# The two value products of an attention tile on two column halves of TensorE, their parts summed at the head's end

## The chip, the cores and the metric

One NeuronCore of a Trainium2 chip runs the program. The metric is the device time of one execution in microseconds. The engines are named as in the profile: PE is TensorE (PEld its weight loads), DVE VectorE, ACT ScalarE, POOL GpSimd, SP the engine that issues most DMAs.

## The reference, cut to what matters

```python
q, k, v = (split_heads(x @ W + b) for W, b in ((Wq, bq), (Wk, bk), (Wv, bv)))   # B=2, L=4096, 16 heads of 16
scores = einsum('bhqd,bhkd->bhqk', q, k) * scale
sparsity = scores.max(-1) - scores.mean(-1)
_, top_idx = top_k(sparsity, 307)
q_sel = take_along_axis(q, top_idx)                       # 307 queries a head
attn = softmax(einsum('bhud,bhkd->bhuk', q_sel, k) * scale)
out_sel = einsum('bhuk,bhkd->bhud', attn, v)              # the two value products
out = zeros_like(q).at[bi, hi, top_idx].set(out_sel)
x = layernorm(x + out.reshape(b, l, D) @ Wo + bo)
x = layernorm(x + rwkv_channel_mix(x))                    # a small gated feed-forward block
```

There are 32 heads in all (two batches of 16). Each has a full score pass, whose row maxima pick 307 queries, and then an attention pass for those 307 over all 4096 keys.

## The kernel before

**The score pass** of a head takes 64 steps. In each, PE makes 128 queries by 2048 scores: one 512-column product into bank `C0` (L782, issued ahead as "lead"), one into `C1` (L791), and two into a half of `DP` (L801). ACT takes absolute values of `C0` and `C1` into `AB` (L1035, two a step), and one DVE instruction adds `DP` and `AB` and keeps the maximum (L1185, followed by the read of its accumulator). `C0` and `C1` have one buffer each, so PE may write the next L782 only when ACT has read the last. 2048 such steps run from about 63 to 2943 us.

**The attention pass** of a head takes 32 tiles of 128 keys. For a tile PE makes 128 keys by 307 scores in bank `B` (L862), ACT takes the exponential into `E` in f32 (L1064), and POOL (or DVE in the last stretch) writes `EL`, what is left of `E` beyond its upper 16 bits. `EH` is a bf16 view of these upper bits. Six tiles later PE multiplies both by the same values: `v` holds 16 columns of the f16 upper part of V, 16 of its lower part and one column of ones. Both products add up in the one bank `PV`, over all 32 tiles:

```python
v = V[hx // H][0][:, (kc * H + h) * VW:(kc * H + h) * VW + 128]
pe.matmul(PV[:, 0:U], v, EH[a % NE], start=kc == 0, stop=False)
pe.matmul(PV[:, 0:U], v, EL[a % NE], start=False, stop=kc == NT - 1).then_inc(pv_pe, 1)
```

The 128 columns of `v` are 33 useful ones and 95 of neighbouring heads, whose results nobody reads.

**The head's end**: ACT copies 33 rows of `PV` to `OT` (L1071), PE transposes them in three pieces (L887), DVE takes the reciprocal of the ones' row, adds the two value parts and multiplies (L1353, L1354, L1356, L1359), and POOL adds the bias and scatters the rows to `AO`.

**The order of the work** is written out ahead by `schedule()`: one list of tokens that every engine walks through, each doing its own part. One score step takes one step of the selection (`sel`: flip, 16 rounds of compare and count, ranks, indices) and one step of the attention. In the steady part PE's order is L782 (next step), L877, L878, L791, L801 twice, L862. Selection steps hold the attention back for a step or two, so a head whose tiles fall into a search takes more score steps. After the last score step ("tail") the attention of the last heads runs alone, and then the feed-forward block of the second batch.

One place outside the attention matters for the reading. The product of the selection's indices (`idx`, L850) has 32 products with `n * 20` columns of weights: 100 for groups of five heads, 60 for groups of three.

Of the kernel before, what the change touches and what calls it, by code (L numbers as in the profile page):

```python
# [9 lines left out]
ALU = mybir.AluOpType  # L10
ACT = mybir.ActivationFunctionType

NB, L, D, H, DH = 2, 4096, 256, 16, 16
NT = L // 128
U = max(1, min(512, int(0.6 * 512)))
# [12 lines left out]
NE = 10  # L28
# [10 lines left out]
def after(engine, semaphore, value):  # L39

    if value > 0:
        engine.wait_ge(semaphore, value)
# [392 lines left out]
def attention_rwkv(nc, x, Wq, bq, Wk, bk, Wv, bv, Wo, bo, W_r, W_k, W_v, mu_r, mu_k, out):  # L435
    ctx = ExitStack()
    with ctx:
        def sb(name, shape, dt=F32):
            return ctx.enter_context(nc.sbuf_tensor(name, shape, dt))

        def sem(name):
            return ctx.enter_context(nc.semaphore(name))
# [8 lines left out]
        VW = 2 * DH + 1  # L451
# [4 lines left out]
        V = [(VF, VS), (XT, XV.rearrange("p t (h d) -> p t h d", d=VW))]  # L456
# [6 lines left out]
        EH = [E[i][:].bitcast(BF16).rearrange("p (u w) -> p u w", w=2)[:, :, 1] for i in range(NE)]  # L463
        W2 = {n: sb("W_" + n, [128, 2, D]) for n in ("k", "o", "rT", "kT", "vT")}
        WH = {n: (sb(f"W{n}h", [128, 2, D], F16), sb(f"W{n}l", [128, 2, D], F16)) for n in ("k", "q", "v")}
        ident = sb("ident", [128, 128])
# [26 lines left out]
        EL = [SCR[:, 6936 + 154 * i:7090 + 154 * i].bitcast(F16)[:, 0:U] for i in range(NE)]  # L493
# [36 lines left out]
        idxs = [sb(f"idxs{i}", [128, HM, 3], I32) for i in range(len(GROUPS))]  # L530
        MH = sb("MH", [128, 24])
        QT = [sb(f"QT{i}", [128, 384], F16) for i in range(2)]
        OT = [sb(f"OT{i}", [2 * DH + 1, 384]) for i in range(2)]
        rec = sb("rec", [128, 3])
        osum = sb("osum", [128, 3, DH])
        OG = [sb(f"OG{i}", [128, 3, DH]) for i in range(2)]

        FF = VF[:, 0:NT * H * VW].bitcast(F32)
# [2 lines left out]
        def ff_tiles(count, w=D):  # L541
# [17 lines left out]
        PV = ctx.enter_context(nc.psum_tensor("PV", [128, 512], F32))  # L559
        DP = ctx.enter_context(nc.psum_tensor("DP", [128, 2, 1024], F32))  # L560
        BANK = {"C0": CP[:, 0, :], "C1": CP[:, 1, :], "B": BP[:], "P": PV[:], "D0": DP[:, 0, :], "D1": DP[:, 1, :],
                "D00": DP[:, 0, 0:512], "D01": DP[:, 0, 512:1024], "D10": DP[:, 1, 0:512], "D11": DP[:, 1, 512:1024]}
# [26 lines left out]
        pv_pe, ot_act, ot_pe, og_dve = (sem(n) for n in ("pv_pe", "ot_act", "ot_pe", "og_dve"))  # L589
# [11 lines left out]
        for token in plan:  # L601
            if token[0] == "st":
                a = (HEAD0[token[1]] + token[2]) * NT + token[3]
# [70 lines left out]
        def _(pe):  # L674
            owed = {}

            def claim(bank):
                banks = {"D0": ("D0", "D00", "D01"), "D1": ("D1", "D10", "D11"), "D00": ("D00", "D0"), "D01": ("D01", "D0"),
                         "D10": ("D10", "D1"), "D11": ("D11", "D1")}.get(bank, (bank,))
                for b in banks:  # L680
                    for s, v in owed.pop(b, ()):
                        pe.wait_ge(s, v)
                return BANK[bank]
# [182 lines left out]
            def pv(g, hl, kc):  # L866
                hx = HEAD0[g] + hl
                a, h = hx * NT + kc, hx % H
                if kc == 0:
                    claim("P")  # L870
                    pe.wait_ge(val_pool, 32 * (hx // H + 1))
                    if hx // H:
                        pe.wait_ge(vones_pool, 1)
                on, count = low[a]
                pe.wait_ge(el_of[on], count)
                v = V[hx // H][0][:, (kc * H + h) * VW:(kc * H + h) * VW + 128]
                pe.matmul(PV[:, 0:U], v, EH[a % NE], start=kc == 0, stop=False)  # L877
                pe.matmul(PV[:, 0:U], v, EL[a % NE], start=False,  # L878
                          stop=kc == NT - 1).then_inc(pv_pe, 1)
                owed["P"] = ((ot_act, hx + 1),)  # L880

            def otr(g, hl, bank):
                hx = HEAD0[g] + hl
                o = claim(bank)
                pe.wait_ge(ot_act, hx + 1)
                for c in range(3):
                    r = pe.transpose(o[:, 64 * c:64 * c + 2 * DH + 1], OT[hx % 2][:, 128 * c:128 * c + 128],  # L887
                                     ident[0:2 * DH + 1, 0:2 * DH + 1])
                r.then_inc(ot_pe, 1)
                owed[bank] = ((og_dve, hx + 1),)  # L890

# [49 lines left out]
            def f7(b, t, c, bank, late):  # L941
# [5 lines left out]
                if c == 1:  # L947
                    r.then_inc(f_v, 1)
                    owed[bank] = ((f_o1, k + 1),)

            stages = dict(xt=xt, kbar=kbar, ffw=ffw, kmm=kmm, qmm=qmm, qtr=qtr, val=val, lead=lead_, second=second, main=main, flip=flip, cnt=cnt, cut=cut, rank=rank,
                          idx=idx, st=st, pv=pv, otr=otr, f1=f1, f2=f2, f4=f4, f6=f6, f6k=f6k, f7=f7)
            for stage, *args in plan:
                if stage in stages:
# [3 lines left out]
        def _(act):  # L958
            seq = Seq(q_act)
# [106 lines left out]
            def fin(g, hl):  # L1066
                hx = HEAD0[g] + hl
                after(act, ot_pe, hx - 1)
                act.wait_ge(consts, 2)
                act.wait_ge(pv_pe, NT * (hx + 1))  # L1070
                act.copy(OT[hx % 2][:, 0:U], PV[0:2 * DH + 1, 0:U]).then_inc(ot_act, 1)  # L1071

            def f1(b, t, bank, late):
                k = NT * b + t
# [37 lines left out]
            def f6k(b, t, part, bank, late):  # L1112
# [6 lines left out]
                if late:  # L1119
                    after(act, f_v, k - 1)  # L1120
                    act.wait_ge(f_rl, k + 1)
                    act.activation(fk2[k % 2], fk[k % 2], ACT.Square).then_inc(f_sq, 1)

            stages = dict(xtev=xtev, ffw=ffw, kev=kev, split=split, qev=qev, qtev=qtev, vev=vev, main=main, flip=flip, cmp=cmp, st=st, fin=fin,
                          f1=f1, f2s=f2s, f4=f4, f6=f6, f6k=f6k)
            for stage, *args in plan:
# [4 lines left out]
        def _(dve):  # L1131
            seq = Seq(q_dve)
# [214 lines left out]

            def otr(g, hl, bank):
                hx = HEAD0[g] + hl
                sv = BANK[bank][:, 0:192].rearrange("p (c d) -> p c d", c=3)  # L1350
                dve.wait_ge(ot_pe, hx + 1)
                after(dve, og_dve, hx)
                dve.reciprocal(rec[:], sv[:, :, 2 * DH])  # L1353
                q = seq.mark(dve.tensor_copy(osum[:], sv[:, :, 0:DH]))  # L1354
                dve.wait_ge(q_dve, q)
                q = seq.mark(dve.tensor_tensor(osum[:], osum[:], sv[:, :, DH:2 * DH], ALU.add))  # L1356
                dve.wait_ge(q_dve, q)
                after(dve, l_o[hx % 2], 48 * (hx // 2))
                dve.tensor_tensor(OG[hx % 2][:], osum[:], rec[:].unsqueeze(2).broadcast_to([128, 3, DH]),  # L1359
                                  ALU.mult).then_inc(og_dve, 1)  # L1360
# [67 lines left out]
            def f9(b, t, late):  # L1428
                if late:
# [6 lines left out]
            stages = dict(xtev=xtev, kbar=kbar, kev=kev, split=split, main=main, cap=capture, parts=parts, cmp=cmp,  # L1436
                          digit=digit, cut=cut, cum=cum, rank=rank, pick=pick, slots=slots, ob=ob, oa=oa, idx=idx,
                          st=st, otr=otr, f2=f2, f3=f3, f5=f5, f7=f7, f8=f8, f9=f9)
            for stage, *args in plan:
                if stage in stages:  # L1440
# [3 lines left out]
        def _(pool):  # L1444
# [5 lines left out]
            def setup():  # L1450
# [23 lines left out]
                for i in range(2):  # L1474
                    q = seq.mark(pool.memset(OT[i][:], 1.0))
                pool.wait_ge(q_pool, q)
# [198 lines left out]
            def put(g, hl):  # L1675
# [5 lines left out]
                pool.wait_ge(og_dve, hx + 1)  # L1681
                pool.wait_ge(q_pool, seq.mark(pool.tensor_tensor(OG[i][:], OG[i][:], bv3, ALU.add)))
                pool.wait_ge(l_z, 256)
                for c, (_, w) in enumerate(CH):
                    k = 3 * hl + c
                    pool.indirect_dma_start(  # L1686
                        out=AOr[b], out_offset=bass.IndirectOffsetOnAxis(ap=ixf[0:w, k:k + 1], axis=0),
                        in_=OG[i][0:w, c, :], in_offset=None).then_inc(l_o[i], 16)

# [262 lines left out]
```

## Time and profile before

| | us |
|---|---|
| median of 3 runs | 3242.62 (3241.13 to 3245.9) |
| profiled execution, its time | 3246.53 |
| profiled execution, its span | 3244.8 |
| PE busy | 2945.3 (91%) |
| DVE busy | 2894.6 (89%) |
| ACT busy | 2821.5 (87%) |
| POOL busy | 1611.0 (50%) |

The span is from the first instruction to the last. A matmul's duration in the profile is modelled and includes the way through the array, so that back-to-back matmuls overlap in the rows. What a matmul costs is read from the distance of its start to the start of the next one: 0.22 us for 512 columns, 0.13 for 307, at full clock.

### The profile page before, as it was taken

The numbers are of one execution on the slowest core, as the hardware profiler recorded it, in microseconds if no ns is written. First come the engines' busy times: TensorE is split into PE (matmuls) and PEld (weight loads), VectorE is DVE, ScalarE is ACT, GpSimd is POOL, SyncE is SP. The second block draws the span as 40 slices with busy tenths as digits, with TensorE's granted clock in tenths as the row PEclk, the third lists the DMA queues.
The fourth block names the chain that finished last, engine by engine and source line by source line (L and its number), as shares of the span: only waits on it lengthen the run. The fifth ranks groups of instructions, "written<-read, shape, count | busy, mean of one in ns | idle before, by whom it ended". The sixth has DMA issues, their size and how long they took to land. (4 is left out here: it accounts for less than half of the span.)

```text
span 3244.8 us, 56078 instructions
## 1 busy us (share of the span) xinstructions
PE 2945.3 (91%) x14524; PEld 1334.2 (41%) x14524; DVE 2894.6 (89%) x5704; ACT 2821.5 (87%) x6214; POOL 1611.0 (50%) x2867
## 2 busy tenths in 40 slices
PE   6999899998999999999899999899998799897588
PEld 3333333333433433443343444444444343344376
DVE  4999999999989998998999999899998698997567
ACT  5999898998999999999899888799997699895476
POOL 4223022224645554653364566766546464657754
PEclk8999999999999999999999999999999999998889
DMA  6324223241251242123111252122241212202122
GB/s 183 92 84 119 74 72 86 86 41 34 44 42 29 37 42 36 21 39 36 35 37 44 51 46 51 38 39 36 42 48 38 46 33 20 42 17 16 19 84 74
DMA packets 276909, 166.61 MB, mean 51 GB/s; under 512 B 182188, under 2 KB 256108, under 8 KB 272492
## 3 DMA queue, kind: packets, MB, share of 16 engines
q1 hardware_dynamic: 268492, 159.56, 26.0%
q0 software_dynamic: 6144, 1.37, 0.5%
q8 instruction: 117, 1.92, 0.3%
q10 hardware_dynamic: 1952, 2.10, 0.2%
q14 instruction: 204, 1.67, 0.2%
HBM read 111.86 MB, written 47.86 MB: 49 GB/s over the span
## 5 line engine op out<-in xcount | busy, mean ns | idle before, releaser
L1185 DVE CUSTOM_DVE_ANT_0 JK<-DP,AB 128x1024 bf16<-128x1024 f32 x2048 | 2459.6, 1222 | 215.2 <-DVE SPr L1185 88.6
L1035 ACT ACTIVATE AB<-CP 128x512 f32<-128x512 f32 x4096 | 2292.1, 623 | 188.5 <-PE CP L782 131.1
L801 PE MATMUL DP<-KS,QS 128*128 128x512 f16 x4096 | 1233.5, 383 | 69.1 <-DVE SPr L1185 60.8
L1673 POOL TENSOR_TENSOR SCR<-E 128x307 f16<-128x307 f32 x957 | 665.1, 708 | 491.4 <-ACT E L1064 485.4
L782 PE MATMUL CP<-KS,QS 128*128 128x512 f16 x2048 | 791.4, 386 | 56.3 <-ACT AB L1035 33.0
L791 PE MATMUL CP<-KS,QS 128*128 128x512 f16 x2048 | 792.2, 387 | 36.3 <-ACT AB L1035 0.2
L801 PEld LDWEIGHTS DP<-KS,QS 128*128 128x128 f16 x4096 | 354.4, 99 | 368.7 <-DVE SPr L1185 179.1
L1064 ACT ACTIVATE E<-BP 128x307 f32<-128x307 f32 x896 | 428.5, 478 | 40.3 <-PE BP L862 34.4
L782 PEld LDWEIGHTS CP<-KS,QS 128*128 128x128 f16 x2048 | 197.6, 96 | 532.8 <-ACT AB L1035 457.9
L791 PEld LDWEIGHTS CP<-KS,QS 128*128 128x128 f16 x2048 | 196.8, 96 | 421.1 <-ACT AB L1035 375.2
L862 PE MATMUL BP<-QT,KA 128*128 128x307 f16 x896 | 265.7, 297 | 12.4 <-DMA QT<-SCR 8.6
L1448 POOL TENSOR_SCALAR SCR<-SCR 128x48 f16<-128x48 f16 (+2 forms) x122 | 50.1, 410 | 388.1 <-ACT SCR L1013 190.9
L1185 DVE DVE_READ_ACCUMULATOR2_ANT SPr<- 128x1 f32 x2048 | 168.1, 82 | 0.0
L877 PE MATMUL PV<-E,XT 128*128 128x307 bf16 x512 | 158.8, 311 | 6.6 <-POOL SCR L1673 6.2
L878 PE MATMUL PV<-SCR,XT 128*128 128x307 f16 x512 | 155.3, 304 | 0.0
L877 PE MATMUL PV<-E,VF 128*128 128x307 bf16 x512 | 153.0, 299 | 0.0
L878 PE MATMUL PV<-SCR,VF 128*128 128x307 f16 x512 | 149.6, 292 | 0.0
L862 PEld LDWEIGHTS BP<-QT,KA 128*128 128x128 f16 x896 | 88.0, 98 | 142.9 <-ACT E L1064 27.5
L1646 POOL DMA_INDIRECT SCR<-QN,idxs x96 | 99.5, 1037 | 70.5 <-DMA idxs<-IDX 34.3
L1686 POOL DMA_INDIRECT AO<-OG,idxs x96 | 100.5, 1047 | 33.9 <-issue 20.5
L1064 ACT ACTIVATE E<-DP 128x307 f32<-128x307 f32 x100 | 40.9, 429 | 51.8 <-PE DP L862 48.5
L1711 POOL TENSOR_SCALAR frs<-fmv 128x1 f32<-128x1 f32 x64 | 14.1, 220 | 136.4 <-DVE fmv L1369 135.9
(411 smaller groups left out, 3016.9 us busy)
## 6 DMA issues: line engine op xcount, KB each, us to landing
KS<-KTC SPq DMA_DIRECT2D x256, 128.0 KB
QS<-QSC SPq DMA_DIRECT2D x512, 64.0 KB
KA<-KTC SPq DMA_DIRECT2D x128, 128.0 KB
QN<-SCR SPq DMA_DIRECT2D x16, 544.0 KB, 3.4
SCR<-in_L_attn_x SPq DMA_DIRECT2D x16, 512.0 KB, 5.1
AO<-E SPq DMA_DIRECT2D x16, 512.0 KB, 6.8
VF<-in_L_attn_x SPq DMA_DIRECT2D x64, 128.0 KB, 2.1
VF<-AO SPq DMA_DIRECT2D x64, 128.0 KB, 2.2
```

The costliest lines, as they stand in the source:

```text
L782: pe.matmul(o, qs, ks[0][:, 1, :], start=True, stop=True).then_inc(sc_c, 1)
L791: pe.matmul(o, qs, ks[1][:, 1, :], start=True, stop=True).then_inc(sc_c, 1)
L801: r = pe.matmul(o[:, 512 * j:512 * j + 512], qs, ks[j][:, 0, :], start=True, stop=True)
L862: pe.matmul(o[:, 0:U], KA[hx % 2][:, 128 * kc:128 * kc + 128], QT[hx % 2][:, 0:U], start=True, stop=True).then_inc(s_pe, 1)
L877: pe.matmul(PV[:, 0:U], v, EH[a % NE], start=kc == 0, stop=False)
L878: pe.matmul(PV[:, 0:U], v, EL[a % NE], start=False, stop=kc == NT - 1).then_inc(pv_pe, 1)
L1035: act.activation(AB[p % 3][:, 512 * j:512 * j + 512], BANK["C%d" % j], ACT.Abs).then_inc(ab_full, 1)
L1064: act.activation(E[a % NE][:], BANK[bank][:, 0:U], ACT.Exp, scale=2 * SCALE / (WS * WS)).then_inc(ex_act, 1)
L1185: dve.tensor_tensor_reduce(out=JK[p % 2][:], in0=BANK["D%d" % u], in1=AB[p % 3][:], scale=1.0, scalar=0.0, op0=ALU.add, op1=ALU.max, accum ...
L1646: pool.indirect_dma_start(out=QG[0:w, 3 * (hx % 8) + c, :], out_offset=None, in_=QNr[b], in_offset=bass.IndirectOffsetOnAxis(ap=ixf[0:w, k ...
L1673: pool.tensor_tensor(EL[a % NE], E[a % NE][:], EH[a % NE], ALU.subtract).then_inc(el_g, 1)
L1686: pool.indirect_dma_start(out=AOr[b], out_offset=bass.IndirectOffsetOnAxis(ap=ixf[0:w, k:k + 1], axis=0), in_=OG[i][0:w, c, :], in_offset= ...
```

## The change

The two value products of a tile no longer add up in the same rows. Each takes 64 columns of weights instead of 128. The product with `EH` goes to rows 0 to 63 of `PV`, the one with `EL` to rows 64 to 127, each accumulated over the 32 tiles by itself. At the head's end ACT copies all 128 rows, PE transposes 128 rows (three products of 128 columns instead of 33), and DVE sums what were one denominator and two value parts from two denominators and four value parts. `rec` now comes from `den`.

```diff
-        OT = [sb(f"OT{i}", [2 * DH + 1, 384]) for i in range(2)]
+        OT = [sb(f"OT{i}", [128, 384]) for i in range(2)]
+        den = sb("den", [128, 3])
...
-                v = V[hx // H][0][:, (kc * H + h) * VW:(kc * H + h) * VW + 128]
-                pe.matmul(PV[:, 0:U], v, EH[a % NE], start=kc == 0, stop=False)
-                pe.matmul(PV[:, 0:U], v, EL[a % NE], start=False,
-                          stop=kc == NT - 1).then_inc(pv_pe, 1)
+                v = V[hx // H][0][:, (kc * H + h) * VW:(kc * H + h) * VW + 64]
+                pe.matmul(PV[0:64, 0:U], v, EH[a % NE], start=kc == 0, stop=kc == NT - 1)
+                pe.matmul(PV[64:128, 0:U], v, EL[a % NE], start=kc == 0, stop=kc == NT - 1).then_inc(pv_pe, 1)
...
-                    r = pe.transpose(o[:, 64 * c:64 * c + 2 * DH + 1], OT[hx % 2][:, 128 * c:128 * c + 128],
-                                     ident[0:2 * DH + 1, 0:2 * DH + 1])
+                    r = pe.transpose(o[:, 128 * c:128 * c + 128], OT[hx % 2][:, 128 * c:128 * c + 128], ident[:])
...
-                act.copy(OT[hx % 2][:, 0:U], PV[0:2 * DH + 1, 0:U]).then_inc(ot_act, 1)
+                act.copy(OT[hx % 2][:, 0:U], PV[:, 0:U]).then_inc(ot_act, 1)
...
-                sv = BANK[bank][:, 0:192].rearrange("p (c d) -> p c d", c=3)
+                sv = BANK[bank][:, 0:384].rearrange("p (c a e) -> p c a e", c=3, a=2)
+                parts = sv[:, :, :, 0:2 * DH].rearrange("p c a (b d) -> p c d a b", d=DH)
                 dve.wait_ge(ot_pe, hx + 1)
                 after(dve, og_dve, hx)
-                dve.reciprocal(rec[:], sv[:, :, 2 * DH])
-                q = seq.mark(dve.tensor_copy(osum[:], sv[:, :, 0:DH]))
+                q = seq.mark(dve.reduce_sum(den[:], sv[:, :, :, 2 * DH], mybir.AxisListType.X))
+                dve.reduce_sum(osum[:], parts, mybir.AxisListType.XY)
                 dve.wait_ge(q_dve, q)
-                q = seq.mark(dve.tensor_tensor(osum[:], osum[:], sv[:, :, DH:2 * DH], ALU.add))
+                q = seq.mark(dve.reciprocal(rec[:], den[:]))
```

No instruction changes its place, and the number of instructions of each engine stays. On PE, in a steady score step with attention, these rows stood before (columns of weights by columns streamed; `E` and `SCR` are `EH` and `EL`, `VF` is V of the first batch):

```order
L782 MATMUL CP<-KS,QS 128x512
L877 MATMUL PV<-E,VF 128x307
L878 MATMUL PV<-SCR,VF 128x307
L791 MATMUL CP<-KS,QS 128x512
L801 MATMUL DP<-KS,QS 128x512 x2
```

The same place of PE's program after the change (one line was added to the file above it, so each line number is one higher):

```order
L783 MATMUL CP<-KS,QS 128x512
L878 MATMUL PV<-E,VF 64x307
L879 MATMUL PV<-SCR,VF 64x307
L792 MATMUL CP<-KS,QS 128x512
L802 MATMUL DP<-KS,QS 128x512 x2
```

Nothing moved: the two value products stand between the same two score products, now with 64 columns of weights while their neighbours have 128.

On DVE, at a head's end, these four rows stood before (`BP` is the bank with the transposed `OT`):

```order
L1353 RECIPROCAL rec<-BP 128x3
L1354 COPY osum<-BP 128x48
L1356 TENSOR_TENSOR osum<-osum,BP 128x48
L1359 TENSOR_TENSOR OG<-osum,rec 128x48
```

The same place on DVE after the change:

```order
L1353 TENSOR_REDUCE den<-BP 128x3
L1354 TENSOR_REDUCE osum<-BP 128x48
L1356 RECIPROCAL rec<-den 128x3
L1359 TENSOR_TENSOR OG<-osum,rec 128x48
```

Four small instructions remain four; two of them now reduce out of PSUM, and the reciprocal comes after the sum.

## Rows read from the trace of the kernel before

**Rows 1.** Busy time by engine: five steady heads, then a head during a search

```profile
2102.60:2327.40 224.80, 223.16 (x1175) 95.62 (x1175) 212.76 (x359) 221.73 (x504) 138.38 (x211) 1.00 0.23 42
1219.00:1286.50 67.50, 63.50 (x307) 24.64 (x306) 59.78 (x137) 65.02 (x148) 28.23 (x49) 1.00 0.10 19
```

**Rows 2.** The same view for L1185 alone, in the second stretch

```profile
1219.00:1286.50 67.50, 55.29 (x92) 1.00 0.10 19
```

**Rows 3.** Timeline of one steady score step with attention: start, duration, engine, line

```profile
2908.11 0.29 PE L862 MATMUL BP<-QT,KA 128*128 128x307 f16 x1
2908.26 0.39 PE L782 MATMUL CP<-KS,QS 128*128 128x512 f16 x1
2908.48 0.30 PE L877 MATMUL PV<-E,XT 128*128 128x307 bf16 x1
2908.50 0.51 ACT L1064 ACTIVATE E<-BP 128x307 f32<-128x307 f32 x1
...
2908.62 0.29 PE L878 MATMUL PV<-SCR,XT 128*128 128x307 f16 x1
...
2908.75 0.39 PE L791 MATMUL CP<-KS,QS 128*128 128x512 f16 x1
2908.82 1.17 ACT L1035 ACTIVATE AB<-CP 128x512 f32<-128x512 f32 x2
2908.82 1.22 DVE L1185 CUSTOM_DVE_ANT_0 JK<-DP,AB 128x1024 bf16<-128x1024 f32 x1
2908.97 0.59 PE L801 MATMUL DP<-KS,QS 128*128 128x512 f16 x2
...
2909.41 0.29 PE L862 MATMUL BP<-QT,KA 128*128 128x307 f16 x1
```

**Rows 4.** L877 alone by stretch: PE busy (x tiles), weight loads, granted clock

```profile
821.00:1763.00 942.00, 152.71 (x511) 50.34 (x511) 1.00 0.25 36
2103.00:2943.00 840.00, 106.42 (x355) 35.06 (x355) 0.98 0.23 36
2943.00:3080.00 137.00, 52.34 (x157) 16.59 (x157) 0.80 0.21 17
```

**Rows 5.** PE's timeline around an index product with 100 columns of weights

```profile
791.39 0.60 PE L801 MATMUL DP<-KS,QS 128*128 128x512 f16 x2
791.83 1.76 PE L850 MATMUL BP<-SCR 128*100 128x80 f16 x32
793.43 0.38 PE L782 MATMUL CP<-KS,QS 128*128 128x512 f16 x1
```

**Rows 6.** PE's timeline around an index product with 60 columns of weights

```profile
1601.62 0.60 PE L801 MATMUL DP<-KS,QS 128*128 128x512 f16 x2
1602.15 1.36 PE L850 MATMUL PV<-SCR 128*60 128x48 f16 x32
1603.45 0.39 PE L782 MATMUL CP<-KS,QS 128*128 128x512 f16 x1
```

**Rows 7.** PE's timeline in the tail, at half clock and then at full

```profile
3028.44 0.46 PE L877 MATMUL PV<-E,XT 128*128 128x307 bf16 x1
...
3029.21 0.46 PE L877 MATMUL PV<-E,XT 128*128 128x307 bf16 x1
...
3032.92 0.30 PE L877 MATMUL PV<-E,XT 128*128 128x307 bf16 x1
3033.05 0.29 PE L878 MATMUL PV<-SCR,XT 128*128 128x307 f16 x1
...
3033.31 0.30 PE L877 MATMUL PV<-E,XT 128*128 128x307 bf16 x1
```

**Rows 8.** A head's end: OT's transposes, osum's copy, and 128-column transposes elsewhere

```profile
L887 PE MATMUL BP<-ident,OT x87: 217/224/248, 864.3 to 3078.6; 33*128 33x33 f32 x87
L1354 DVE COPY osum<-BP x29: 165/176/179, 866.0 to 3079.0; 128x48 f32<-128x48 f32 x29
L687 PE MATMUL PV<-ident,SCR 128*128 128x128 f32 x100 | 16.8, 295 | 9.8 <-DMA SCR<-in_L_attn_x 7.6 <-issue 2.1
```

## The prediction

> **What bounds the kernel now.** I read the busy time by stretch first, then the timeline of single steps. Over five steady attention heads PE is busy 223.16 of 224.80 us, ACT 221.73 and DVE 212.76, at granted clock 1.00 (the 2.4 GHz level) [rows 1]. The reader is to see that three engines are nearly full there, and PE fullest. Busy matmul time is modelled and overlaps, so I check it in the timeline [rows 3]: from L862 to the next L862 is 1.30 us, and PE's starts follow each other without a hole: 0.15 (L862 to L782), 0.22 (to L877), 0.14 (to L878), 0.13 (to L791), 0.22 (to L801), 0.44 (two L801). A 307-column product needs 0.13 and a 512-column one about 0.22, so all that is slack in 1.30 us is some 0.02 before L782, 0.01 in the L877 distance and little else. Whatever is added to PE in such a step is added to the step, less about 0.02.
>
> Where a search runs, it is different: 67.50 us for a head's 32 tiles [rows 1], with 92 rows of L1185 [rows 2], two a step, so 46 steps of 1.47 us. Here steps without a tile and waits of the search lie between, and part of an addition disappears in them.
>
> Tiles by stretch: 511 + 355 = 866 beside score steps, and 157 in the tail, where the granted clock averages 0.80 [rows 4] (one record is missing from 1024). In the tail the score steps are gone and PE often sets the pace alone: a tile takes 3033.31 - 3032.92 = 0.39 at full clock, which is three products of 0.13, and 3029.21 - 3028.44 = 0.77 at half clock [rows 7].
>
> **The change, part by part.** *The pair itself.* Before, both products stream one after the other through the whole array: 0.14 + 0.13 = 0.27 [rows 3]. Two halves of the array could stream them together. From below, the second starts with the first and the pair costs 0.13 (-0.14); from above, they still go one after the other and cost 0.27 (0). I take a value near the lower bound: the second starts one weight load later. The nearest row is the 60-column index product, whose 32 loads and products follow each other at (1603.45 - 1602.15 - 0.10)/32 = 0.04 [rows 6]. So the pair costs 0.04 + 0.13 = 0.17, a gain of 0.10. No row here shows two halves working at once.
>
> *Entering and leaving the half-width form.* PE goes from 128 columns of weights to 64 and back in every tile. The index product does the same with 60 columns and, for the larger groups, not with 100. With 100 columns L801's pair to L850 is 791.83 - 791.39 = 0.44, two plain 512-column distances [rows 5]; with 60 it is 1602.15 - 1601.62 = 0.53 [rows 6]. Entering costs 0.09. Leaving: the 60-column group ends at 1602.15 + 1.36 = 1603.51, its last product is about 0.19 long, so it starts at 1603.32, and L782 follows 0.13 later, though 48 columns stream in 0.02 at the rate of rows 3 (0.13 for 307). With 100 columns the same distance is 793.59 - 0.21 = 793.38 to 793.43, 0.05. Leaving thus costs 0.08 to 0.11; I take 0.10. That is 0.19 a tile, seen in every row pair of this kind and to be hidden only where PE waits anyway. On this the Trainium skill (TensorEngine Tiling (Array Packing), Key Properties) says that changing the tiling mode, and not only the tile, drains TensorE. By that rule each tile pays twice; the trace agrees, with 0.09 and 0.10 us. The page gives no price.
>
> *Sum for a steady step.* 0.19 - 0.10 = +0.09 on the stretch from L782 to L791, +0.01 as the weight load of L791 can't run ahead, -0.02 of slack: +0.08, from 1.30 to 1.38. Sixteen of the 27 heads beside score steps run like the first stretch of rows 1, about 512 tiles: 512 x 0.08 = 41 us. The other 354 tiles lie in searches; I count half: 14. Together 55.
>
> *Tail.* A tile goes from 0.39 to 0.13 + 0.09 + 0.04 + 0.13 + 0.10 = 0.49, +0.10. About half of 157 tiles are paced by PE at full clock (80 x 0.10 = 8), some 25 at half clock with twice the price (5): 13.
>
> *The head's end, 32 times.* PE's three transposes take 128 columns of f32 instead of 33: modelled durations 295 against 224 ns [rows 8], at most +0.21 a head, 7 us; but the 33-row form seems to be entered and left at a price too, about 0.19, 6 us, and goes. I take 0, and -6 to +7 as its ends. DVE: a copy is 176 ns [rows 8]; two copy-like instructions become reductions over 6 and 192 elements. From 0 to one more copy's time each, 0 to 11 us in all, hidden behind PE except where PE waits for the bank; I take 2. ACT's copy of 128 rows instead of 33 has the same 307 elements a row: 0. If the cover of the last head is gone, these are a few tenths of a us.
>
> Nothing else moves: POOL, the DMAs and every wait stay.
>
> Sum: 55 + 13 + 2 = 70; I take 66, since ACT and DVE get slack and catch up after searches. Against the profiled execution that is 3246.53 + 66 = 3313. The median of the runs is 3.9 lower: 3309. Since a pair somewhat shorter than I took it is as likely as not, I say 3305, which is +62.
>
> **Rivals.** *One after the other (0.17).* The halves don't overlap. The pair stays at 0.27 and both entries are paid in full: +0.19 - 0.02 = +0.17 a step. (512 + 177) x 0.17 = 117, tail 80 x 0.19 + 25 x 0.38 = 25: +142, 3385. For it: the second product's weights are loaded only after the first has been issued. Against: nothing makes the second product wait for the first.
>
> *Faster (0.05).* Entering and leaving costs nothing beside long neighbours, because the 0.09 and 0.10 of the index product come from its short products, and only the overlap is left: -0.10 to -0.14 a tile. It decides where the switch price falls under 0.10. ACT (221.73 of 224.80 [rows 1]) then sets the step, so that only 0.02 is gained in 689 steps (14), and in the tail 80 x 0.08 = 6: -20, 3223. Against: the 0.09 of entering follows a 512-column product, just as here [rows 6]. The Trainium skill (TensorEngine Tiling (Array Packing), Theoretical Speedup) gives up to two times for products with at most 64 columns of weights, which points this way; by that rule alone the pair would cost 0.13. Here it is the mechanism of this rival without the switches, and no row before shows it.
>
> *No difference (0.04).* The switches cost about what the overlap gives (-0.14 + 0.16), and the slack of 0.02 hides it: 3242.6.
>
> *The clock (0.05).* Twice 0.1 us without a stream in each 1.4 us step, and the granted clock, 1.00 in steady heads [rows 1], falls to half as it does in the tail [rows 4]. Every twentieth of the 1780 us of attention beside score steps at half clock costs nearly as much again, some 60 to 80 us: 3380 and more. Against: in the search head of rows 1 PE also pauses (63.50 of 67.50 us busy) and the granted clock stays at 1.00.
>
> *As forecast, two switches and an overlap (0.69).* Its own range: second product at once and other slack, +0.04 a step: 28 + 8 = +36, less the head's end, +25 at the lowest, 3268; second product 0.08 later and all of it exposed, +0.12: 83 + 17 = +100, 3340.
>
> **How the numbers follow.** The range has to reach from the lowest of the forecast's cases into the serial rival, whose own low end is about 3350 and middle 3385: 3262 to 3385 leaves out some 0.09 below (faster, none) and 0.09 above. A difference of 0.2% (6.5 us) is about what a measurement of this kernel can tell from none. Faster 0.05, same 0.04, slower 0.91 (0.69 + 0.17 + 0.05).
>
> **What the changed profile would show.** Right: L783 to L792, 0.49 before, is about 0.59; L783 to L878 is 0.31, L878 to L879 is 0.04 or less, L879 to L792 0.23; the steady step is 1.38, with PE's distances leaving no hole and holes appearing on DVE and ACT; in the tail a tile at full clock takes 0.49. Serial rival: L878 to L879 0.13 or more. Faster rival: L783 to L878 stays at 0.22. Clock rival: the granted clock of steady heads under 1.00. The prediction would be wrong most easily in the distance from L878 to L879, for which I have only a neighbour's rows, and next in how much of the addition the searches hide.

## The result: 1.6% slower, and the profile after

| | us |
|---|---|
| before, median of 4 runs | 3243.14 (3241.13 to 3245.9) |
| changed, median of 4 runs | 3294.93 (3289.77 to 3303.08) |
| ratio, with its 95% interval | 1.0157 (1.0133 to 1.0182) |
| changed, profiled execution and its span | 3290.62, 3288.9 |

The change costs 52 us. The profiled execution lies 4.3 below the median and before's 3.4 above it, so that the changed span is only 44.1 longer.

The timeline of PE in a steady step of the changed kernel (start, duration, engine, line), to be held against [rows 3]:

```profile
2240.75 0.29 PE L863 MATMUL BP<-QT,KA 128*128 128x307 f16 x1
2240.88 0.38 PE L783 MATMUL CP<-KS,QS 128*128 128x512 f16 x1
2241.19 0.33 PE L878 MATMUL PV<-E,XT 128*64 128x307 bf16 x1
2241.20 0.32 PE L879 MATMUL PV<-SCR,XT 128*64 128x307 f16 x1
2241.45 0.39 PE L792 MATMUL CP<-KS,QS 128*128 128x512 f16 x1
2241.68 0.59 PE L802 MATMUL DP<-KS,QS 128*128 128x512 f16 x2
2242.11 0.29 PE L863 MATMUL BP<-QT,KA 128*128 128x307 f16 x1
```

The two value products now start 0.01 apart instead of 0.14: the halves stream together. But the first starts 0.31 after L783 instead of 0.22, and L792 starts 0.25 after the second instead of 0.13. From L783 to L792 it is 0.57 instead of 0.49, and the step takes 1.36 instead of 1.30.

Busy time by stretch: its length, then PE, weight loads, DVE, ACT, POOL, then granted clock, DMA share and GB/s. First the five steady heads and the search head of [rows 1], then the tail.

```profile
2120.40:2353.80 233.40, 232.23 (x1174) 87.21 (x1175) 213.56 (x361) 229.88 (x504) 138.48 (x211) 1.00 0.23 41
1226.97:1294.66 67.69, 64.10 (x307) 23.43 (x306) 59.80 (x139) 65.31 (x149) 28.28 (x49) 1.00 0.17 19
2971.00:3124.00 153.00, 113.38 (x549) 43.68 (x549) 79.56 (x216) 65.21 (x157) 103.11 (x164) 0.61 0.24 15
```

The same view of before's tail:

```profile
2943.00:3078.00 135.00, 87.12 (x549) 53.69 (x549) 86.71 (x214) 62.63 (x157) 104.30 (x164) 0.80 0.22 17
```

Five steady heads take 233.40 instead of 224.80 us, 0.054 for each of their 160 tiles. PE is still the fullest engine, at full clock, and DVE has done the same work in more time. The search head, from the start of its first tile to the end of its last, takes 67.69 instead of 67.50, under 0.01 for each of its 32 tiles. The tail grows from 135.0 to 153.0, and its granted clock falls from 0.80 to 0.61.

The score pass by its first and last instruction on DVE, before and then changed (duration min/median/max, first and last start):

```profile
L1185 DVE CUSTOM_DVE_ANT_0 JK<-DP,AB x2048: 1204/1223/1270, 63.6 to 2941.5; 128x1024 bf16<-128x1024 f32 x187
```

```profile
L1184 DVE CUSTOM_DVE_ANT_0 JK<-DP,AB x2048: 1201/1224/1273, 65.5 to 2969.8; 128x1024 bf16<-128x1024 f32 x187
```

It lasts 2904.3 instead of 2877.9 us: +26.4. The start is 1.9 later, the tail is 18 longer, and what follows the tail is some 2 shorter. That makes up the 44. Taken head by head, from a head's first value product to its last, the 26 is made of +28.0 in the sixteen heads without a search (0.055 a tile), +5.6 in ten of the eleven whose tiles fall into a search (0.018 a tile), -5.9 in the eleventh, +1.1 between the heads and -2.4 ahead of the first tile.

The -5.9 doesn't come from the change. Before, one subtraction of DVE took 4.79 us in that head, while POOL worked without a pause beside it:

```profile
2793.70 4.79 DVE L1324 TENSOR_TENSOR SCR<-fa,numbers 128x192 f16<-128x192 f16 x1
```

In the changed kernel it takes 0.35. It is as long in two more kernels with the old form there (`cols96`, `head_end`) and short in two others with the old form there (`tail_only`, `tail_all`), so it is chance that before's profile has it. Without it the score pass would be some 32 us longer, not 26.

The tail of the changed kernel on PE, at half clock and then at full:

```profile
3060.72 0.44 PE L878 MATMUL PV<-E,XT 128*64 128x307 bf16 x1
3060.72 0.47 PE L879 MATMUL PV<-SCR,XT 128*64 128x307 f16 x1
3061.12 0.44 PE L863 MATMUL CP<-QT,KA 128*128 128x307 f16 x1
3061.49 0.47 PE L878 MATMUL PV<-E,XT 128*64 128x307 bf16 x1
...
3062.22 0.32 PE L878 MATMUL PV<-E,XT 128*64 128x307 bf16 x1
...
3062.72 0.33 PE L878 MATMUL PV<-E,XT 128*64 128x307 bf16 x1
```

At full clock a tile takes 0.50 (3062.22 to 3062.72) against 0.39 [rows 7]. At half clock it takes 0.77, exactly as before. Over the tail's distances from tile to tile, before had 80 at 0.39 to 0.42 and 27 at 0.76 to 1.0; now 44 are at 0.43 to 0.50 and 75 at 0.76 to 1.0.

The head's end, changed: DVE's four rows (busy us, mean ns).

```profile
L1353 DVE TENSOR_REDUCE den<-BP 128x3 f32<-128x6 f32 x29 | 4.6, 159 | 2.4 <-PE BP L887 2.1 <-issue 0.3
L1354 DVE TENSOR_REDUCE osum<-BP 128x48 f32<-128x192 f32 x29 | 10.1, 348 | 0.0
L1356 DVE RECIPROCAL rec<-den 128x3 f32<-128x3 f32 x32 | 5.3, 166 | 0.0
L1359 DVE TENSOR_TENSOR OG<-osum,rec 128x48 f32<-128x48 f32 x32 | 6.7, 210 | 1.2
```

The sum over 192 elements takes 348 ns where the copy took 176 [rows 8], and the others are 14 to 37 ns shorter: with before's 174 + 176 + 203 + 224 = 777 in the same view, 883 now, +0.1 us a head. On PE it is the other way round: from the product ahead of the three transposes to the one behind them it takes 0.54 us instead of 0.61 (medians of 27 heads).

### The profile page after: what moved, and what is told of

Same layout as the page of the kernel before. It is cut to its first block and busy times, and to the rows that moved or that the text cites. A ratio compares the mean times of both kernels' runs of the same rounds, so it can differ in the third digit from the quotient of the medians.

```text
span 3288.9 us, 56078 instructions
## 1 busy us (share of the span) xinstructions
PE 3014.1 (92%) x14524; PEld 1280.5 (39%) x14524; DVE 2884.8 (88%) x5704; ACT 2859.9 (87%) x6214; POOL 1608.6 (49%) x2867
## 3 DMA queue, kind: packets, MB, share of 16 engines
q8 instruction: 117, 1.92, 0.3%
## 5 line engine op out<-in xcount | busy, mean ns | idle before, releaser
L1034 ACT ACTIVATE AB<-CP 128x512 f32<-128x512 f32 x4096 | 2250.5, 602 | 186.4 <-PE CP L783 126.3
L783 PE MATMUL CP<-KS,QS 128*128 128x512 f16 x2048 | 785.8, 384 | 53.4 <-ACT AB L1034 32.8
L792 PE MATMUL CP<-KS,QS 128*128 128x512 f16 x2048 | 797.6, 389 | 36.0 <-ACT AB L1034 0.6
L1063 ACT ACTIVATE E<-BP 128x307 f32<-128x307 f32 x896 | 385.3, 430 | 37.1 <-PE BP L863 30.3
L783 PEld LDWEIGHTS CP<-KS,QS 128*128 128x128 f16 x2048 | 198.6, 97 | 444.6 <-ACT AB L1034 318.6
L792 PEld LDWEIGHTS CP<-KS,QS 128*128 128x128 f16 x2048 | 196.8, 96 | 433.6 <-ACT AB L1034 291.8
L878 PE MATMUL PV<-E,XT 128*64 128x307 bf16 x512 | 179.2, 354 | 2.9 <-POOL SCR L1673 2.9
L879 PE MATMUL PV<-SCR,XT 128*64 128x307 f16 x512 | 176.7, 349 | 0.0
L878 PE MATMUL PV<-E,VF 128*64 128x307 bf16 x512 | 166.7, 326 | 0.0
L879 PE MATMUL PV<-SCR,VF 128*64 128x307 f16 x512 | 163.2, 319 | 0.0
L878 PEld LDWEIGHTS PV<-E,VF 128*64 128x64 f16 x512 | 54.6, 107 | 160.3 <-POOL SCR L1673 93.6
L878 PEld LDWEIGHTS PV<-E,XT 128*64 128x64 f16 x512 | 57.2, 112 | 152.7 <-POOL SCR L1673 85.3
```

Source lines behind the costliest of these rows:

```text
L783: pe.matmul(o, qs, ks[0][:, 1, :], start=True, stop=True).then_inc(sc_c, 1)
L792: pe.matmul(o, qs, ks[1][:, 1, :], start=True, stop=True).then_inc(sc_c, 1)
L878: pe.matmul(PV[0:64, 0:U], v, EH[a % NE], start=kc == 0, stop=kc == NT - 1)
L879: pe.matmul(PV[64:128, 0:U], v, EL[a % NE], start=kc == 0, stop=kc == NT - 1).then_inc(pv_pe, 1)
L1034: act.activation(AB[p % 3][:, 512 * j:512 * j + 512], BANK["C%d" % j], ACT.Abs).then_inc(ab_full, 1)
L1063: act.activation(E[a % NE][:], BANK[bank][:, 0:U], ACT.Exp, scale=2 * SCALE / (WS * WS)).then_inc(ex_act, 1)
```

## The experiments

### One half, and the width alone

`one_half` keeps 64 columns of weights, but puts both products into the same half, as before into one sum. `cols96` takes 96 columns. Both have the old head's end. Product rows of `one_half`, with 64 for 96 the only difference to `cols96`:

```diff
-                v = V[...][:, (kc * H + h) * VW:(kc * H + h) * VW + 128]
-                pe.matmul(PV[:, 0:U], v, EH[a % NE], start=kc == 0, stop=False)
-                pe.matmul(PV[:, 0:U], v, EL[a % NE], start=False,
+                v = V[...][:, (kc * H + h) * VW:(kc * H + h) * VW + 64]
+                pe.matmul(PV[0:64, 0:U], v, EH[a % NE], start=kc == 0, stop=False)
+                pe.matmul(PV[0:64, 0:U], v, EL[a % NE], start=False,
```

Expected of `one_half`: 

> Both products with 64 columns of weights, but both into rows 0 to 63 of PV, so that the form is entered and left as in the change and nothing can overlap. My theory (two paid switches, 0.09 and 0.13 us, and a gain of 0.13 from two halves streaming at once): L877 to L878 0.13 to 0.14 us, L782 to L877 0.31, L878 to L791 0.255, steady step 1.49 us, total about +165 us, 3410. Rival (the halves gain nothing, the loss comes from the form alone): the same total as the change, 3295. Rival (the chip overlaps two products of one half as well): distance L877 to L878 far under 0.13.

Expected of `cols96`: 

> Both products with 96 columns of weights into rows 0 to 95, added up as before. If a change of form (array split in halves) is what costs, 96 columns are still the full form: distances 0.226, 0.138 and 0.130 us and total as before, 3243 within 6 us. Rival (any width other than the neighbours' 128 costs a load that cannot run ahead): L782 to L877 0.31 and a total of +100 us or more, since nothing overlaps.

Measured: `one_half` 1.0434 (1.0416 to 1.0451), `cols96` 0.9999 (0.9984 to 1.0014). The steady step of `one_half` is 1.485, as expected, and its total, 3379, is 31 below what was expected. PE's timeline of `one_half`, then of `cols96`:

```profile
2288.62 0.38 PE L782 MATMUL CP<-KS,QS 128*128 128x512 f16 x1
2288.93 0.32 PE L877 MATMUL PV<-E,XT 128*64 128x307 bf16 x1
2289.09 0.29 PE L878 MATMUL PV<-SCR,XT 128*64 128x307 f16 x1
2289.32 0.39 PE L791 MATMUL CP<-KS,QS 128*128 128x512 f16 x1
```

```profile
2289.47 0.38 PE L782 MATMUL CP<-KS,QS 128*128 128x512 f16 x1
2289.69 0.30 PE L877 MATMUL PV<-E,XT 128*96 128x307 bf16 x1
2289.83 0.29 PE L878 MATMUL PV<-SCR,XT 128*96 128x307 f16 x1
2289.96 0.38 PE L791 MATMUL CP<-KS,QS 128*128 128x512 f16 x1
```

With 96 columns every distance is that of before, and so is the time: the price belongs to the 64-column form. In one half, entering costs the same 0.31, the second product starts 0.16 after the first, and L791 follows 0.23 later: 0.70 from L782 to L791. This is the serial rival: its score pass is 110 us longer than before's, and its tail 157 us long. Against it the overlap gains 0.70 - 0.57 = 0.13 a tile, a whole product, and 1.0434 - 1.0157 = 2.8% of the time. So the overlap is real, and the change loses in spite of it.

### Beside the score steps, and in the tail

`beside_only` has the change for heads 0 to 26 and the old form for the last five, whose tiles fill the tail. `tail_only` is the reverse. `tail_all` is `tail_only` with the tile's score product (L862) in two halves too, so that in the tail PE never leaves the form within a head.

```diff
+def halved(hx):
+    return hx < 27          # beside_only; hx >= 27 in tail_only and tail_all
...
+                if halved(hx):      # tail_all only
+                    for m in (0, 64):
+                        r = pe.matmul(o[m:m + 64, 0:U], KA[hx % 2][:, 128 * kc + m:128 * kc + m + 64], QT[hx % 2][:, 0:U],
+                                      start=True, stop=True)
```

Expected of `beside_only`: 

> The change for heads 0 to 26 (beside score steps) and the old form for the last five heads (tail). If the change costs PE 0.055 us in a steady step and nearly nothing in a search: +27 us, 3270, with the tail as before at 135 us. Rival (the tail is longer because of what comes ahead of it, not because of its own products): total as the change, 3295.

Expected of `tail_only`: 

> The other part: the old form for heads 0 to 26 and the change for the last five heads (the tail). In the changed kernel the tail was 17 us longer than before and at half clock for 108 us instead of 55. If the tail's own products do that: steady steps 1.30 us, the tail 150 us long with about 105 us at half clock, total +18, 3261. Rival (the tail's clock was chance): tail 135 to 140 us, total within 5 us of before.

Expected of `tail_all`: 

> As before for heads 0 to 26; for the last five heads the value products on two halves and the score product of the tile (L862) too, as two products of 64 columns into rows 0 to 63 and 64 to 127, so that PE stays in the half form from tile to tile. Paid switches: none left between tiles, a tile takes 0.13 + 0.13 = 0.27 us at full clock and 0.51 at half, ACT (0.31 to 0.40) or POOL and DVE (0.35) set the pace, tail 115 to 125 us, total 3225 to 3235. Rival (POOL, DVE and the waits set the tail, or the clock stays at half): tail as before, 3243.

Measured: `beside_only` 1.0100 (1.0083 to 1.0117), `tail_only` 1.0062 (1.0039 to 1.0085), `tail_all` 0.9997 (0.9984 to 1.0011). The two parts add up to 1.0162, the change's 1.0157. `beside_only` costs 27 to 38 us by its interval, where 27 had been expected; `tail_only` came as expected in size (20 us against 18), and for `tail_all` the rival held, not the forecast. The tail by stretch, of `beside_only`, `tail_only` and `tail_all`:

```profile
2968.60:3103.50 134.90, 88.22 (x549) 52.43 (x549) 85.43 (x216) 62.81 (x157) 104.84 (x164) 0.80 0.21 17
```

```profile
2934.50:3097.00 162.50, 126.71 (x549) 45.26 (x549) 79.19 (x216) 66.14 (x157) 102.35 (x164) 0.52 0.16 14
```

```profile
2940.50:3075.00 134.50, 78.72 (x702) 46.42 (x703) 86.16 (x214) 58.82 (x157) 103.29 (x164) 0.72 0.25 17
```

With the old form in the tail the granted clock is 0.80 and the tail 134.9, as before. With the change it is 0.52 in one profile and 0.61 in the other, and the tail is 162.5 and 153.0. The tail's loss goes with the clock, in the ten executions of `tail_only` too: 3249 to 3256 us where the granted clock of the whole was 0.966 to 0.968, 3260 to 3276 where it was 0.958 to 0.963. Without the switches (`tail_all`) the clock is 0.72, the tail has its old length and nothing is gained, though PE is busy for 78.72 instead of 87.12 us. Its tiles at full clock are mostly no longer paced by PE: POOL's and DVE's subtractions stand next, with POOL busy for 103.29 of 134.50 us and PE waiting 10.0 us for POOL's (L1707) where it waited 6.6 before.

### The head's end alone

`head_end` has before's two products and the change's head's end. Since the rows 64 to 127 then hold other heads' columns, its sums add rows that don't belong to them, and its output is not the reference's.

```diff
-                v = V[...][:, (kc * H + h) * VW:(kc * H + h) * VW + 64]
-                pe.matmul(PV[0:64, 0:U], v, EH[a % NE], start=kc == 0, stop=kc == NT - 1)
-                pe.matmul(PV[64:128, 0:U], v, EL[a % NE], start=kc == 0, stop=kc == NT - 1).then_inc(pv_pe, 1)
+                v = V[...][:, (kc * H + h) * VW:(kc * H + h) * VW + 128]
+                pe.matmul(PV[:, 0:U], v, EH[a % NE], start=kc == 0, stop=False)
+                pe.matmul(PV[:, 0:U], v, EL[a % NE], start=False, stop=kc == NT - 1).then_inc(pv_pe, 1)
```

Expected: 

> The value products as before and the change's head end alone (copy of 128 rows, three 128-column transposes, two reductions); its output adds rows twice over, so only its time counts. I expect nothing measurable: 3243 within 5 us, PE's stay in the transposes 0.22 + 3 x 0.11 against 0.31 + 0.15 + 0.16 us before. Rival: the reductions out of PSUM hold the bank, PE waits for it, 0.2 us a head, +6.

Measured: 1.0010 (0.9992 to 1.0028). Anything from -3 to +9 us fits, and 2 had been forecast. No more can be said of so small a term.

### Two and four tiles together

If the switches are the cost, fewer of them should cost less. `pairs` issues the value products of two tiles in every second attention step, `fours` those of four in every fourth. `pairs_full` is `pairs` with before's 128 columns: it pays for the grouping alone.

```diff
-            if j >= 0:
-                step.append(("pv", g, j // NT, j % NT))
+            if j >= 0 and j % 2 == 1:
+                for m in range(j - 1, j + 1):
+                    step.append(("pv", g, m // NT, m % NT))
```

Expected of `pairs`: 

> The change, with the value products of two tiles together in every second step, so that half the switches go. Theory of paid switches: one stay in the half form of two tiles costs PE 0.09 + 0.13 + 0.13 + 0.13 = 0.48 us in two steps, against 0.54 before and 1.13 less score work in the change; steady steps average 1.28 to 1.30 us, total 3235 to 3250. Rival (0.48 us without score products starve ACT, which has one buffer for each half of its input): steady steps average 1.33 us or more, total 3270.

Expected of `fours`: 

> The change with the value products of four tiles together in every fourth step. PE spends 0.09 + 4 x 0.13 + 0.13 = 0.74 us in four steps against 1.07 before, so that ACT (about 1.26 us a step) would be the bound: 3225 if the steps stay even. Rival (starvation): while PE is away for 0.74 us ACT runs out of input and the fourth step takes 1.6 us or more: mean 1.34, 3275.

Expected of `pairs_full`: 

> The kernel before, with its value products in the full form but for two tiles together in every second step. The change grouped in this way lost 45 us although it has half the switches. If the grouping itself costs (a light step of 1.00 us of PE work, which ACT with 1.26 cannot follow, and a heavy one of 1.54, in which ACT runs dry): two steps take 1.26 to 1.30 + 1.54 = about 2.8 us against 2.60, total +50 to +80, 3290 to 3320. Rival (buffers even it out, and the grouped change lost by its switches alone): as before, 3240.

Measured: `pairs` 1.0136 (1.0119 to 1.0153), `fours` 1.0224 (1.0195 to 1.0253), `pairs_full` 1.0154 (1.0131 to 1.0177). The forecast for `pairs_full` held; those for `pairs` and `fours` failed, and their rival, starvation, came, with larger totals (3283 and 3311) than it had been given. The old form, grouped, loses as much as the change does. Two steps of `pairs_full`, by the starts of L792:

```profile
2222.77 0.38 PE L792 MATMUL CP<-KS,QS 128*128 128x512 f16 x1
...
2223.55 0.38 PE L783 MATMUL CP<-KS,QS 128*128 128x512 f16 x1
2223.90 0.39 PE L792 MATMUL CP<-KS,QS 128*128 128x512 f16 x1
...
2225.54 0.38 PE L792 MATMUL CP<-KS,QS 128*128 128x512 f16 x1
```

A step without value products takes 1.13, one with four 1.64. In the light step PE waits for ACT: L792 starts 0.35 after L783 instead of 0.22, and the trace gives ACT's absolute value as what its weight load waited for, since `C0` and `C1` have one buffer each and nothing can run ahead. So PE's heavy step is exposed and its light one isn't as short as PE could make it. Where the grouping is paid in both, the half form gains little or nothing that is clear of noise: `pairs` against `pairs_full` is 1.0136 against 1.0154 (a difference within their intervals), and the median steady step 1.367 against 1.396 us. By the distances, an entry and an exit cost 0.083 + 0.125 = 0.21 and a pair gains 0.135, so that the form should pay from two pairs on; no total here shows a gain.

### The score products in halves too

The other way to pay for no switch is to never leave the form. `all_half` makes every score product and every L862 of two halves; `half_steps` does so only in score steps that hold value products, and for L862 in the tail.

```diff
+            def halves(o, w, x):
+                for m in (0, 64):
+                    r = pe.matmul(o[m:m + 64, :], w[:, m:m + 64], x, start=True, stop=True)
+                return r
...
-                    r = pe.matmul(o[:, 512 * j:512 * j + 512], qs, ks[j][:, 0, :], start=True, stop=True)
+                    r = halves(o[:, 512 * j:512 * j + 512], qs, ks[j][:, 0, :])
```

Expected of `all_half`: 

> The change, and all score products (L782, L791, L801, L862) too as two products of 64 columns of weights into rows 0 to 63 and 64 to 127, so that PE stays in the half form through a whole step and nothing of the change's saving is paid back. If the switches are the whole loss, and a pair in the half form costs its stream and about 0.03 us for a load that cannot hide (0.155 to 0.163 us for 307 columns were seen in the half form): a step is 4 x 0.25 + 2 x 0.16 = 1.31 us on PE at most, total 3235 to 3260. Rival (the half form itself is slow: twice the instructions, no load ahead of a product): 4 x 0.30 + 2 x 0.20 = 1.60 us a step, +250 us or more.

Expected of `half_steps`: 

> The change, with the score products (L782, L791, L801, L862) in the half form only in the steps that hold value products, and in the tail L862; everything else is in the full form. With every product in halves a steady step took 1.30 us, as before the change, and that kernel lost its 135 us where full products of other stages stood between halves. If the switches are the whole loss: steady steps 1.30, one or two switches a head left, total 3235 to 3250, not to be told from before. If the freed PE time (the step needs some 1.20 us of PE) helped after all: below 3230. Rival (something else in the change costs, the doubled copy or the head's end): 3260 or more.

Measured: `all_half` 1.0421 (1.0402 to 1.0441), `half_steps` 1.0112 (1.0094 to 1.0130). PE's timeline of `all_half` in a steady step, and where a full-width projection stands between score products:

```profile
2222.15 0.41 PE L776 MATMUL CP<-KS,QS 128*64 128x512 f16 x2
2222.39 0.30 PE L882 MATMUL PV<-E,XT 128*64 128x307 bf16 x1
2222.39 0.29 PE L883 MATMUL PV<-SCR,XT 128*64 128x307 f16 x1
2222.64 0.41 PE L776 MATMUL CP<-KS,QS 128*64 128x512 f16 x2
...
2223.45 0.41 PE L776 MATMUL CP<-KS,QS 128*64 128x512 f16 x2
```

```profile
650.47 0.41 PE L776 MATMUL CP<-KS,QS 128*64 128x512 f16 x2
650.81 0.60 PE L724 MATMUL PV<-XT,Wqh 128*128 128x512 f16 x2
651.34 0.41 PE L776 MATMUL CP<-KS,QS 128*64 128x512 f16 x2
```

The forecast of `all_half`, 3235 to 3260, failed with 3380. In the steady step it holds: without switches the pair is free, the step is 1.30 again (2222.15 to 2223.45), L776 follows L776 after 0.49 with the value products between them, as L791 followed L782 before [rows 3]. It isn't under 1.30; ACT, 221.73 of 224.80 us busy before [rows 1], is next. The time is lost elsewhere. Part of it is the switches around full-width products: 0.34 into L724 and 0.53 for its two products and out again (at full width such distances are 0.22 and 0.43). The first and last value product and score instruction of `all_half`:

```profile
L1188 DVE CUSTOM_DVE_ANT_0 JK<-DP,AB x2048: 1201/1225/1244, 60.9 to 3069.5; 128x1024 bf16<-128x1024 f32 x187
...
L882 PE MATMUL PV<-E,VF x512: 296/301/305, 874.2 to 1843.4; 128*64 128x307 bf16 x171
```

From the first score step to the first value product it is 813 us, where the change has 820.9 - 65.5 = 755: +58 with no attention running. PE changes its form 831 times in that stretch, and not once before the change, so 0.07 us for each, an estimate near the price of a switch, would be enough. `half_steps` leaves these steps alone, and its median steady step is 1.30 too, but its score pass is 38 us longer than before's (60.5 to 2976.7). In the sixteen heads without a search 26 steps take over 1.6 us, where 4 did before. One of them, on PE, with what POOL did then:

```profile
2224.01 1.07 POOL L1705 DMA_INDIRECT AO<-OG,idxs  x1 [0.30 <-issue]
2224.37 0.60 PE L789 MATMUL DP<-KS,QS 128*64 128x512 f16 x4
2225.44 0.32 PE L789 MATMUL BP<-QT,KA 128*64 128x307 f16 x2 [0.47 <-issue]
```

PE stood idle for 0.47 us and waited for nothing that the trace shows. The forecast of no loss failed here, and the rival's time (3260 or more) came without the rival's cause, since `head_end` has the doubled copy and the new head's end at 1.0010.

The trace says where these stalls lie. From the first tile to the end of the score pass `half_steps` has 20 of more than 0.25 us without a releaser and `all_half` 19, and every one of them lies during or within 0.3 us behind an indirect DMA of POOL (a gather of `QN` or a scatter into `AO`), though these rows cover only 8% of the time. In the sixteen heads the steps beside such a DMA take 1.61 us on average in `half_steps` and 1.64 in `all_half`, all others 1.30; before, both kinds take 1.30. These 72 steps of `half_steps` times 0.31 are the 23 us by which its sixteen heads are longer. So the loss there isn't one of switches or of the form in general. (The 18 us that it loses in ten heads beside searches were not taken apart.) What an indirect DMA withholds from PE is not shown. These kernels give PE more instructions, and their instruction queue moved 2.47 and 3.08 MB where before moved 1.92, so it could be the supply of instructions; no run separated this.

## Why the prediction was right

**What bounds the kernel: right.** PE's addition became the step's. Of +0.073 from L783 to L792 (medians, 0.494 to 0.567), 0.056 reached the step, with 0.02 of slack taken up as forecast.

**The pair: the direction right, the size beyond what was taken.** The second product was put 0.04 after the first; it starts 0.003 after it (median), with its weights loaded beside those of the first. The overlap is complete and gains 0.135, not 0.10. The Trainium skill (TensorE: Matmul & The Clock Gate, Part 3) gives about 4 ns between the starts of packed products; this trace agrees, with 3 ns.

**Entering and leaving: right, one of them too low.** Entering was taken as 0.09 from the 60-column index product, and 0.309 - 0.226 = 0.083 was measured. The weight loads show what changed. In the full form L877's is started as soon as L782 streams, 0.22 ahead of its product; in the change it comes only with the product:

```profile
2908.27 0.10 PEld L877 LDWEIGHTS PV<-E,XT 128*128 128x128 f16 x1
```

```profile
2241.19 0.11 PEld L878 LDWEIGHTS PV<-E,XT 128*64 128x64 f16 x1 [0.34 <-POOL SCR L1673]
```

The POOL instruction named there ended 0.14 us earlier and works for a later tile; where none is named, the distance is 0.309 as well.

Leaving was taken as 0.10; L879 to L792 is 0.255, and a whole product is 0.13, so it costs 0.125. In `one_half` the distance to L791 is only 0.224, 0.094 over the product; why leaving costs 0.03 less there is not shown. The errors lie on different sides: -0.035 for the overlap, -0.007 for entering, +0.015 for leaving (with the 0.01 that had been set aside for a weight load), and +0.08 a step became +0.056.

**The sum beside score steps: too high, 55 against 26 in the profiles and 27 to 38 by `beside_only`.** For the 512 steady tiles 41 had been forecast; 28.0 was measured, 0.055 a tile. For the tiles beside searches half of the addition had been counted, 14 in all; ten of these eleven heads show 5.6, 0.018 a tile, so that waits cover about two thirds of it. The eleventh is the one with the 4.79 us subtraction before, whose -5.9 is luck. (The record said to be missing from 1024 isn't: it lies just behind the first window of [rows 4].)

**The tail: the sum right, the cause wrong.** 13 was forecast, and 18 measured. It was to come from 0.10 a tile at full clock and twice that at half clock. At full clock it is 0.10, for 44 tiles: 4. At half clock it is nothing, 0.77 before and after. This is the step of the tail's sum that failed: the overlap does save twice as much there (0.258 against 0.134), but the switches don't cost twice as much. Entering and leaving take 0.105 + 0.125 = 0.23 at full clock and 0.115 + 0.147 = 0.26 at half; `one_half`, which has nothing but the switches and the delayed second product, loses 0.225 a tile at full clock and 0.254 at half. The rest is that more tiles run at half clock: 75 - 27 = 48 of them, each 0.38 longer than at full clock, 18. Together 22, of which some was slack. This is the clock rival, which I had priced for the score steps, where it didn't come (granted clock 1.00), and not for the tail, where it did. That 13 and 18 lie so close is luck. The tail as a whole costs 0.6% by `tail_only`.

**The head's end: as forecast,** as far as can be told: +0.1 us of DVE a head, PE's transposes without a switch and 0.07 shorter, 1.0010 with no clear sign.

**The total.** +52 against +62: the score steps came 17 to 28 us lower than their 55 and the tail 5 higher than its 13, and 8 had been taken off the sum of 70. The direction and the size rest on the two prices and the overlap, each of which was measured within 0.035 of what was forecast.

**The rivals.** Serial: excluded by the 3 ns, and `one_half` shows its price, +142 us by the medians (3236.8 to 3378.6), which is the +142 worked out for it (117 and 25; the profile has 110 in the score pass and 22 in the tail). Faster: excluded, the switch price beside long neighbours is that of the short ones. What decided the sign was the price of the form, read from an unrelated product of 60 columns in the same trace; all three such products beside score steps start 0.309 after the one ahead, the very distance of the change.

## What to carry to other kernels

Two products on two column halves really run together, but what counts is what stands beside them: PE pays some 0.08 us to enter the 64-column form and 0.10 to 0.13 to leave it, and the overlap of one pair of 307 columns (0.13) doesn't earn that back. Count the pairs per excursion, not the pairs: by these prices two would earn a little, as long as grouping them costs nothing, which here it did. At half clock one pair breaks even, since the overlap doubles and the switches hardly grow (0.23 to 0.26). If some product in the trace already changes its form, its neighbours' distances price the switch before anything is built; and in a stretch where the granted clock already wavers, expect a change of PE's rhythm to move the clock too.

## What the runs showed of the hardware that was not expected

- In the 64-column form two products that follow each other in one half start 0.163 us apart and not 0.138 (`one_half`). The second's weight load starts 0.026 after the first product instead of 0.002, which is the difference, and takes 110 ns instead of 98. With 96 columns the loads take 123 to 130 ns, and it costs nothing.
- The granted clock of the tail was 0.80 to 0.82 in five kernels with 128 or 96 columns of weights there, 0.61 and 0.52 with the change, 0.71 in `one_half`, and 0.69 to 0.72 with everything in halves or with grouped pairs (five kernels). What makes the chip choose the lower level is open.
- Kernels with more and shorter products on PE (18,872 in `half_steps` and 23,740 in `all_half` against 14,524) stalled for 0.3 to 1.2 us without a releaser, each time beside an indirect DMA of POOL. With the old number of products such a DMA costs PE nothing (1.30 us a step beside it and away from it). Whether it delays the supply of instructions is open.
- One instruction of DVE can take many times its usual length beside a busy POOL. In the head that became shorter the mean of ten subtractions was 944 ns before and 393 in the changed kernel, but that mean hides one of 4787 ns; of the other nine, five took 349 to 355 and four 687 to 817:

```profile
L1324 DVE TENSOR_TENSOR SCR<-fa,numbers 128x192 f16<-128x192 f16 x10 | 9.4, 944 | 0.0
```

```profile
L1323 DVE TENSOR_TENSOR SCR<-fa,numbers 128x192 f16<-128x192 f16 x10 | 3.9, 393 | 0.0
```
